# A graph transformer layer on one core: routing of tokens cut into small parts, gate logits from raw rows, and no zero product ahead of the window sums

## What is computed

```
xn = layernorm(x)
x = x + gnn(xn, src, dst) + mix(xn)
h = layernorm(x)
x = x + ffn(h)

gnn: alpha = softmax over edges of one source; agg[dst] += feature[src] * alpha; agg @ W_fc.T + b_fc
mix: qkv projection, dots = k_norm.T @ v_norm per head, q @ dots / N, output projection
ffn: logits = h @ gate_w + gate_b
     probs = softmax(logits); idx = argmax(probs); prb = max(probs)
     pos = running count of tokens that chose the same expert, minus 1
     kept = pos < C, C = ceil(1.25 * T / 8)
     token goes to row pos of its expert's buffer; relu(row @ w1 + b1) @ w2 + b2
     y = that row * prb * kept
```

## Time and profile before

| | us |
|---|---|
| median of 3 runs | 2183.7 |
| lowest and highest | 2178.46, 2188.65 |
| span of the profiled execution | 2181.3 |
| median less span | 2.4 |

### The profile page before, as it was taken

The page is one execution under the profiler, slowest core; times in us unless marked ns, Lnnn a source line. Parts: engine busy times, 40 slices in busy tenths (PEclk is TensorE's granted clock), DMA queues, the critical chain, the costliest instruction groups (busy, mean ns, idle before and its releaser), DMA issues. The chain is left out here.

```text
span 2181.3 us, 44890 instructions
## 1 busy us (share of the span) xinstructions
PE 1899.4 (87%) x12055; PEld 1346.6 (62%) x12055; DVE 1486.4 (68%) x6582; ACT 781.6 (36%) x3785; POOL 1223.5 (56%) x1251
## 2 busy tenths in 40 slices
PE   8997888878888888888887899999999679999997
PEld 5654555545555545555544566666666479999996
DVE  7775788878887888788787587666767624343433
ACT  6772444444444444444443011111111123333332
POOL 0006777777777777777774576656766312222222
PEclk9997889889888899899898799889999789999998
DMA  7867888888888888888885898877978566565650
GB/s 238 245 220 208 254 243 253 248 242 242 254 245 241 251 247 250 241 253 250 246 253 165 249 313 264 266 234 254 323 245 259 157 242 200 195 202 191 204 186 28
DMA packets 287974, 507.17 MB, mean 233 GB/s; under 512 B 59024, under 2 KB 199730, under 8 KB 287580
## 3 DMA queue, kind: packets, MB, share of 16 engines
q1 hardware_dynamic: 212556, 279.91, 40.8%
q0 software_dynamic: 75152, 224.23, 34.3%
HBM read 394.78 MB, written 112.83 MB: 233 GB/s over the span
## 5 line engine op out<-in xcount | busy, mean ns | idle before, releaser
L836 POOL DMA_INDIRECT pool_mem<-node_tab,edges x592 | 580.9, 981 | 346.1 <-issue 339.7
L1659 POOL DMA_INDIRECT main<-node_tab,edges x294 | 287.6, 978 | 189.2 <-issue 81.6
L967 PE MATMUL psum<-main 32*128 32x258 f32 x1568 | 217.3, 468 | 76.9 <-DVE main L1088 73.6
L977 PE MATMUL psum<-pool_mem,ident 128*128 128x258 f32 x592 | 201.0, 469 | 34.4 <-DMA pool_mem<-node_tab,edges 34.3
L876 ACT ACTIVATE main<-score_all,neg_max 128x8 f32<-128x8 f32 x98 | 29.6, 302 | 555.0 <-DVE neg_max L1119 555.0
L836 POOL DMA_INDIRECT main<-node_tab,edges x192 | 189.5, 987 | 58.5 <-issue 54.2
L2655 POOL DMA_INDIRECT out_dram<-pool_mem x56 | 56.9, 1016 | 282.3 <-DVE pool_mem L2752 266.6
L2685 PEld LDWEIGHTS psum<-pool_mem,main 128*128 128x128 f32 x1792 | 210.9, 194 | 3.3 <-issue 0.5
L2685 PE MATMUL psum<-pool_mem,main 128*128 128x128 f32 x1792 | 211.3, 277 | 0.1
L1000 PE MATMUL psum<-wkvT,main 128*128 128x512 f32 x392 | 200.6, 637 | 7.8 <-ACT main L886 7.5
L882 ACT ACTIVATE main<-main 128x64 f32<-128x64 f32 x784 | 197.9, 334 | 24.1 <-DVE main L1133 23.6
(11 more groups left out here) (284 smaller groups left out, 3656.8 us busy)
## 6 DMA issues: line engine op xcount, KB each, us to landing
main<-in_L_ffn_w_dram SPq DMA_DIRECT2D x64, 1024.0 KB, 5.4
main<-kept_rows SPq DMA_DIRECT2D x98, 640.0 KB
kept_rows<-pool_mem SPq DMA_DIRECT2D x74, 640.0 KB, 5.5
kept_rows<-main SPq DMA_DIRECT2D x24, 640.0 KB
node_tab<-pool_mem SPq DMA_DIRECT2D x49, 258.0 KB, 3.0
main<-proj_t SPq DMA_DIRECT2D x392, 32.2 KB
pool_mem<-node_tab,edges POOLq DMA_INDIRECT x592
moe_in<-zeros SPq DMA_DIRECT2D x32, 258.0 KB, 3.8
```

The costliest lines, as they stand in the source:

```text
L836: g.indirect_dma_start(source_rows(r, u, ZW + D), None, node_tab, bass.IndirectOffsetOnAxis(ap=edges[:, 0, HALF * k + u:HALF * k + u + 1], ...
L967: mm = pe.matmul(psum[:, Z_BANK[q], 0:ZW], hot_T[h][rows_q, j * P:(j + 1) * P], t_win[rows_q, h, :], start=True, stop=(pair in BY_VECTOR), ...
L977: pe.matmul(psum[:, Z_BANK[u % GROUPS_W], 0:ZW], ident[:, :], source_rows(r, u, ZW), start=False, stop=True).then_inc(s_z, 1)
L1659: g.indirect_dma_start(rows_g[k % R3][:, u - KEEP, 0:n], None, node_tab, bass.IndirectOffsetOnAxis(ap=edges[:, 0, HALF * k + u:HALF * k + ...
```

## The change

It does four things, all in the message pass.

1. `window_sums` no longer multiplies by zeros ahead of the sums.
2. The DVE loop of a step begins with `lows(k+2)`; `alphas(k+1)`, `weights(k+1)`, `places(k)` and `hots(k+2)` follow.
3. Routing of a batch becomes one list of 31 small parts, `route(b, n)`, dealt out over six of seven steps by `ROUTE_OPS`, and within a step over five places between the large instructions (`routing(k, part, 5)`).
4. The logits are computed from the raw rows `xs`, with a gate matrix whose column mean is taken off (`gate_w0`), and multiplied by the inverse deviation afterwards; so `turn` no longer waits for ACT's normalised rows, and TensorE turns one tile every two steps. Some algebra of the routing is shortened, tables that all batches share are made once (`route_tables`), and the token and gate columns are written for a whole batch by one instruction each. ACT normalises three tiles per step, and the sends of a batch begin 9 steps after its last half (before: 10 plus its size).

```diff
+        ROUTE_OPS = {2: (0, 6), 3: (6, 12), 4: (12, 16), 5: (16, 21), 6: (21, 23), 7: (23, 23), 8: (23, 31)}
-        LAST_STEP = HALVES + 10 + 2 * SIZES[-1]
+        LAST_STEP = HALVES + 9 + SIZES[-1]
-        HR = 14
+        HR = 2 * G
...
+        def routed(k):
+            return [(b, k - 2 * STARTS[b + 1]) for b in range(BATCHES) if k - 2 * STARTS[b + 1] in ROUTE_OPS]
+        def tile_at(k, offset, pace=1):
+            return [t for t in range(NT) if 2 * STARTS[BATCH_OF[t] + 1] + (t - STARTS[BATCH_OF[t]]) // pace + offset == k]
...
                     def send(t):
-                        wait(g, s_rows_done, 2 * t + 2)
+                        wait(g, s_rows_done, 2 * (BATCH_OF[t] + 1))
...
                         fetch_half(k + R3)
-                        for t in sent_at(k):
+                        for t in tile_at(k, 9):
                             send(t)
...
-                        pe.matmul(psum[:, SUM_BANK[h], 0:D], zeros[:, 0:P], zeros[:, 0:D], start=True, stop=True)
                         for n, slots in enumerate(ROUNDS):
...
                     def turn(t):
-                        wait(pe, s_h, t + 1)
+                        wait(pe, s_xr, t + 1)
...
-                            mm = pe.transpose(psum[:, hT_bank(t), c * P:(c + 1) * P], hrow[:, t % HR, c * P:(c + 1) * P], ident[:, :])
+                            mm = pe.transpose(psum[:, H_BANK, c * P:(c + 1) * P], xs[:, t % XS, c * P:(c + 1) * P], ident[:, :])
...
-                        for t in tile_at(k, 3):
-                            turn(t)
-                        for t in tile_at(k, 5):
-                            logit(t)
-                        for b in tiled(k, 8):
-                            rank(b)
+                        if k % 2 == 0 and 0 <= (k - 4) // 2 < NT:
+                            turn((k - 4) // 2)
+                        if k % 2 == 1 and 0 <= (k - 5) // 2 < NT:
+                            logit((k - 5) // 2)
+                        for b, at_step in routed(k):
+                            if at_step == 7:
+                                rank(b)
...
+                        elif n == 12:
+                            wait(v, s_lg, last)
+                            wait(v, s_re, b)
+                            v.tensor_tensor(logits_n, batch_logits(b).rearrange("p (t e) -> p t e", e=NE), wide(rstd_n), ALU.mult).then_inc(s_lgc, 1)
...
+                        elif n == 23:
+                            wait(v, s_rm, b + 1)
+                            v.tensor_tensor(tmp_n, batch_places(b).rearrange("p (t e) -> p t e", e=NE), chosen_n, ALU.mult).then_inc(s_places, 1)
...
+                    def routing(k, part, parts):
+                        for b, at_step in routed(k):
+                            lo, hi = ROUTE_OPS[at_step]
+                            for n in range(lo + (hi - lo) * part // parts, lo + (hi - lo) * (part + 1) // parts):
+                                route(b, n)
...
+                        if k + 2 < HALVES:
+                            lows(k + 2)
+                        routing(k, 0, 5)
                         if k + 1 < HALVES:
                             alphas(k + 1)
-                        if k + 2 < HALVES:
-                            lows(k + 2)
+                            routing(k, 1, 5)
+                            weights(k + 1)
+                        else:
+                            routing(k, 1, 5)
+                        routing(k, 2, 5)
                         if k < HALVES:
                             places(k)
-                        if k + 1 < HALVES:
-                            weights(k + 1)
+                        routing(k, 3, 5)
                         if k + 2 < HALVES:
                             hots(k + 2)
...
-                        for b in tiled(k, 10):
-                            route_slots(b)
-                        for b in tiled(k, 6):
-                            route_logits(b)
-                        for b in tiled(k, 8):
-                            route_choice(b)
+                        routing(k, 4, 5)
```

More of the change, by code:

```diff
@@ L1416, in graph_transformer_kernel @@
         tmp = m.take(G, NE)
-        seen = m.take(NE)
-        new_seen = m.take(NE)
+        seen = m.take(2, NE)
         new_part = m.take(NE)
@@ L1424, in graph_transformer_kernel @@
         pos = m.take(G)
[L1425 to L1428, removed]
+        place_b = m.take(G)
+        trash_all = m.take(NT)
+        token_all = m.take(NT)
+        share = m.take(NE)
+        gate_w0 = m.take(DC, NE)
         valid = m.take(1)
+        beyond = m.take(1)
         at_fold = m.at
@@ L1671, in _ @@
                         fetch_half(k + R3)
-                        for t in sent_at(k):
+                        for t in tile_at(k, 9):
                             send(t)
                     for i in range(HR):
-                        g.wait_ge(s_sentw[i], 16 * len(range(i, NT, HR)))
+                        g.wait_ge(s_sentw[i], 16 * len([t for t in range(NT) if row_slot(t) == i]))
                     g.wait_ge(s_spread, 2)
@@ L1882, in rank @@
                         wait(pe, s_r, 2 * b + 2)
-                        wait(pe, s_lgc, 2 * b + 1)
+                        wait(pe, s_places, b)
                         n = SIZES[b]
@@ L1886, in rank @@
                         pe.matmul(place, above[:, :], chosen[:, 0:n, :].rearrange("p t e -> p (t e)"), start=True, stop=False)
-                        pe.matmul(place.rearrange("p (t e) -> p t e", e=NE), ones[:, :], seen.unsqueeze(1).to_broadcast([P, n, NE]), start=False, stop=False)
+                        pe.matmul(place.rearrange("p (t e) -> p t e", e=NE), ones[:, :], seen[:, b % 2, :].unsqueeze(1).to_broadcast([P, n, NE]), start=False, stop=False)
                         for i in range(n - 1):
@@ L1893, in _ @@
                     for j in range(2):
-                        mm = pe.matmul(psum[:, ROUTE_BANK, 0:D], ones[0:1, :], bias_row[:, j, :], start=(j == 0), stop=(j == 1))
+                        pe.matmul(psum[:, ROUTE_BANK, 0:D], ones[0:1, :], bias_row[:, j, :], start=(j == 0), stop=(j == 1))
+                    for c in range(DC):
+                        mm = pe.matmul(psum[:, ROUTE_BANK, D:D + NE], ones[:, :], gw[:, c, :], start=(c == 0), stop=(c == DC - 1))
                     mm.then_inc(s_fold, 1)
@@ L2064, in measure, with wide, route @@
                         dve.done(v.bn_aggr(mean_var[:, b % 2, 2 * i:2 * i + 2], stats))
-                    def spread(b, n):
+                    def wide(a):
+                        return a.unsqueeze(2).to_broadcast([P, a.shape[1], NE])
+                    def route(b, n):
+                        tiles, first, last = SIZES[b], STARTS[b], STARTS[b + 1]
+                        slots = slice(b % 2 * G, b % 2 * G + tiles)
+                        logits_n, expos_n, chosen_n, tmp_n = logits[:, 0:tiles, :], expos[:, 0:tiles, :], chosen[:, 0:tiles, :], tmp[:, 0:tiles, :]
+                        red_n, prob_n, expert_n, pos_n, place_n = red[:, 0:tiles], prob[:, 0:tiles], expert[:, 0:tiles], pos[:, 0:tiles], place_b[:, 0:tiles]
+                        rstd_n = rstd[:, b % 2, 0:tiles]
+                        shares = share.unsqueeze(1).to_broadcast([P, tiles, NE])
```

206 lines of the change are left out of this document (101 added, 105 removed).

## The result

The changed kernel takes **2121.0 us** (median of 4 runs, 2116.2 to 2126.2), the kernel before 2183.9 (2183.7 before its fourth run): ratio 0.9703, 95% interval 0.9676 to 0.973. That is 62.9 us less; forecast were 2127 us, in a range of 2106 to 2156.

The account below looks back on a forecast made before the run. No engine was full; queues waited for one another, with POOL's 63.2 us per batch as floor against 73.2. Terms 2.3 + 41 + 3 + 10.5 = 57 us off gave span 2124.5, median 2127 us, range 2106 to 2156.

Parts of the forecast that it names:

- The zero product: Message pass, steps 5 to 19: dropping it takes the stretch from 57.3 to 55 us, 2.3 us off, bounds 0 and 3.4.
- POOL's 42 gathers need 53.9: Steps 5 to 19, without routing: POOL's gathers need 53.9 us of the 57.3, so they limit the gain there.
- Order and small parts: Steps 19 to 89, five batches: both TensorE holes go, a batch falls from 73.2 to 65 us, 41 us off.
- POOL's floor: Per batch of 14 steps, POOL needs 63.2 us for 42 gathers and 7 sends, against the 73.2 they take.
- The 3% on top: Steps 19 to 89: allowance on POOL's 63.2 us for new waits and seven sends in a row, giving 65 per batch.
- Steps 89 to 97: Last steps of the message pass: 37.5 us fall to 34.4, 3 us off, bounds 0 and 4.
- Behind the last sums: From the last sums to the chunk table: 27.4 us fall to 16.8, 10.5 us off, bounds 5 and 14.
- DMA engines: Rival, chance 0.15: they become the bound in steps 19 to 89, a batch takes some 68.5 us, 2148 in all.
- with POOL idle: Condition in the DMA rival's sign: VectorE waits for gathers far over 30 us while POOL is idle.
- The clock: Rival, chance 0.07: TensorE, idle more often, falls to half clock; a batch takes 86 us, 2233 in all, slower.
- Routing's waits: Rival, chance 0.07: waits only change places, steps still stop, a batch stays at 72 us or so, 2171 in all.
- no hole over 1.5 us per batch: Sign that the forecast is right: no hole of TensorE over 1.5 us per batch is left.

Follow-up runs that it names:

- C: The changed kernel, with all four things of the change made to the kernel before: 2121.0 us, ratio 0.9703.
- B: The kernel before the change, against which all ratios are taken: 2183.9 us.
- the pair of experiments: Two edits of C from half 4 on: third gather replaced by a plain load, 2081.5 us; two of five kept tiles not loaded, 2119.0 us.
- sends apart: C with the sends of a batch in every second step instead of seven steps in a row, last two batches unchanged: 2116.7 us, ratio 0.9677.
- six tiles kept: C with sends apart, `lows` late in steps 0 to 4, and six of eight row tiles kept by the second stage: 2101.3 us, ratio 0.962.

## Why the prediction was right, and where it wasn't

The total held: forecast span 2124.5, measured 2124.4. By stretches the profiled execution's 56.9 us are 3.7 + 43.1 + 2.5 + 10.4, less 3.6 lost up to step 5, and 0.8 more gained behind the table. That the spans agree to 0.1 us is luck: against the forecast the terms are off by +1.4, +2, -0.5, -0.1, -3.6 and +0.8 us, and these cancel. The median came out 6 us under 2127 because the profiled execution was the slowest of the four (2126.2, 1.8 over its span).

*The zero product: 2.3 us forecast, 3.7 measured on steps 5 to 19, outside the bound of 3.4.* The step that failed is "POOL's 42 gathers need 53.9". With 28 gathers instead of 42 the stretch still takes 53.6 us: it is TensorE's own need, next to POOL's by chance. And "it isn't worth that" was true of the sum, but not of the edit. Put back into C, the product costs 19 us, 11.5 of them in batches; my sum had that gain under another heading. Nor are the 3.7 us of steps 5 to 19 the product's alone: taken out of B it gives 0.7 there (56.7 us), and with `lows` first 3.6 (56.4 to 52.9).

*Order and small parts: 41 us forecast, 43 measured.* The mechanism, POOL's floor, is shown by the pair of experiments: 38.7 us for a third of the gathers, 1 us for a fifth of the bytes. The 3% on top was a guess of 1.8 us per batch; 64.6 less 63.2 is 1.4, and spreading the sends takes the batch to 63.0. TensorE's need at full clock was put at 53.7 and is some 55.6.

*Steps 89 to 97: 3 forecast, 2.5 measured.* The sums of step 97 wait 3.22 us for their weights.

*Behind the last sums: 10.5 forecast, 10.4 measured, and the terms held too.* VectorE and TensorE there, to be laid beside the earlier trace rows:

```profile
1669.77 0.42 DVE L2061 TENSOR_TENSOR pool_mem<-pool_mem,psum 128x256 f32<-128x256 f32 x1 [0.75 <-PE psum L1839]
```

```profile
1672.54 1.85 PE L1884 MATMUL psum<-pool_mem,ones 128*128 128x32 f32 x8
...
1679.53 0.62 PE L1880 MATMUL psum<-pool_mem,above 128*128 128x24 f32 x2 [3.12 <-DVE pool_mem L2116]
```

3.8 us to the last tile (3 forecast), 4.6 to the end of batch 6's rank (4.7), 5.1 of small parts (5.5), 3.4 to the table at 1682.88 (3.6). The products still run at half clock.

*Nothing at the start.* From the stage's first product to step 5 it was 3.0 us longer, in the spread of 48.8 to 53.1 shown above.

*The rivals.* DMA engines: their signs were there (waits for gathers from 30.0 to 55.9 us, share 0.92), and they were false; the condition "with POOL idle" was the one that decided. The clock: in B without zeros it took all of the gain. In C the mean fell from 0.93 to 0.90, and most of that costs nothing, since POOL is the bound, but not all. Five of C's nine steps over 7 us stand behind the holes described next; a sixth (step 34) stands behind a hole of 1.12 us. The other three, steps 50, 64 and 78, stand right behind a rank, without a hole. TensorE around step 50, this step in the columns of the earlier trace rows, and POOL behind it:

```profile
1447.49 1.58 PE L1884 MATMUL psum<-pool_mem,ones 128*128 128x48 f32 x12
1448.99 1.94 PE L1828 MATMUL psum<-main,pool_mem 128*32 128x256 f32 x16
```

```profile
1448.99:1456.67 7.68, 7.68 (x40) 4.99 (x39) 5.42 (x39) 0.00 (x0) 4.67 (x5) 0.57 0.89 287
```

```profile
1457.61 1.01 POOL L1657 DMA_INDIRECT main<-node_tab,edges  x1 [2.73 <-PE psum L1828]
```

TensorE is busy all the time, at a mean clock of 0.57 (0.56 in the other two), and the step takes 7.68 us in place of 4.57. POOL has to wait for its sums to free a buffer: 2.73, 1.76 and 1.40 us behind these three steps, 3.1 us in all behind step 34. Of the 15.8 us that POOL waits for TensorE in the stretch 7.2 would be issue anyway (24 times 0.3), and of the 8.6 left 7.2 stand in these four places. So most of what C loses over POOL's floor is the clock's price, by the timeline; with sends apart the three steps behind a rank run at full clock, and POOL's waits are gone. Why the clock falls there isn't shown.

Routing's waits: VectorE waits 6.8 us for ranks, 1.4 per batch. The forecast "no hole over 1.5 us per batch" was wrong; there is one group per batch, of 1.25 to 2.90 us, at the same step of every batch, while POOL works through the seven sends. My explanation by the row of seven sends covered only part of it. The group stays with sends apart and with a fifth fewer bytes. With the third gather as a plain load, and with six tiles kept, one step in the 70 is left over 7 us, and with the third gather left out one too. So it is POOL's shortage itself.

Slips of reading that the sum doesn't use: the 18.3 us behind the table are 18.0 (1738.99 to 1757); a step without routing at share 0.98 takes 4.05 us, not 4.03; and behind B's second hole stands a lookup at half clock (2.37 us), not sums of 1.94.

What stays open: how the 54 us of the routing's rewrite divide between small parts and raw rows. No run has the one without the other.

## What to carry to other kernels

When several engines wait for one another, find each one's need per round first, and take the highest as the floor; an edit to any other engine is worth what the present waits let through, which can be nothing alone and 19 us in company. To tell a full queue from full DMA engines, give the same bytes to another queue, and then fewer bytes to the same one. If the queue is the bound, look for a stage before that has the data in hand and spare bandwidth.

## What the runs showed of the hardware

- DMA engines at a busy share of 0.98 and 342 GB/s held next to nothing up (2.8 us of 284), and at 0.92 nothing was gained by 20% fewer bytes. A busy share near one is no proof of a bound. "DMA: Bandwidth & Descriptors" of the Trainium skill (section on where 436 GB/s comes from) ends a core's HBM side near 358 GB/s; the 342 GB/s of the 284 us fit under that. Short windows go over it: 364 GB/s in steps 9 to 11 of the kernel with the plain load (7.65 us), 381 in step 64 of C (7.80 us). So here the 358 are no hard end.
- Taking 41 us of products off TensorE in 70 steps went with a mean clock of 0.84 instead of 0.93 and made them 11.9 us longer. I had expected the clock to matter only if TensorE were the bound; it is enough that it waits more often, in holes of 1.4 to 3.5 us.
- In C TensorE also fell to a clock of 0.56 to 0.57 in three steps that stand behind a rank, with no idle time before them; the twelve products ahead have at most 48 columns (1.58 us).
- An indirect gather of 128 rows of 1 KB holds POOL for 0.968 to 1.012 us in the mean of steps 19 to 89 of every kernel, whether the DMA engines are busy 0.79 or 0.98 of the time, with 0.3 us of issue behind it. That price is steady enough to compute a queue's floor from.
